# First image's state scan of a four-layer kernel: the product of delta*u and B on VectorE from PSUM instead of on GpSimd from a copy

## The reference

```
delta = softplus(dt @ W_dt.T + b_dt)          # 64 channels per pixel
A = -exp(A_log)                               # 64 channels x 16 states
...
dA = exp(d_t[..., None] * A)
h = dA * h + (d_t * u_t)[..., None] * B_t[:, None, :]
y = einsum('bdn,bn->bd', h, C_t)
...
y = (y + u * D) * silu(z)
return y @ W_out.T
```

## Time and profile before

| What | us |
|---|---|
| Three runs, median (lowest to highest) | 1260.89 (1253.15 to 1263.19) |
| Span of the profiled execution, first to last instruction | 1329.2 |
| First image's scan in it, first L1086 to the end of the last gate | 241.37 to 416.08 |
| Second image's scan, first L1026 to the last L1033 | 526.00 to 786.57 |
| First gather | 456.50 |
| Busy in the span: TensorE, VectorE, ScalarE, GpSimd | 611.3, 726.1, 269.3, 747.4 |

### The profile page before, as it was taken

The page is one execution under the profiler, slowest core; times in us unless marked ns, Lnnn a source line. Parts: engine busy times, 40 slices in busy tenths (PEclk is TensorE's granted clock), DMA queues, the critical chain, the costliest instruction groups (busy, mean ns, idle before and its releaser), DMA issues.

```text
span 1329.2 us, 7458 instructions
## 1 busy us (share of the span) xinstructions
PE 611.3 (46%) x1884; PEld 282.5 (21%) x1884; DVE 726.1 (55%) x894; ACT 269.3 (20%) x357; POOL 747.4 (56%) x627
## 2 busy tenths in 40 slices
PE   3414838667665755655657474341114112431115
PEld 1211213222221222222323221131002101220003
DVE  4989435899987556877878784081003101341004
ACT  1110137534441335121212111010001000110001
POOL 0325000444551278787877787567774775677770
PEclk9656879788787885787878786665556655575556
DMA  3000033000000511111111116222111111111110
GB/s 93 0 0 0 0 72 79 0 0 0 0 0 21 124 50 36 46 40 45 41 45 42 45 44 142 72 65 54 51 51 28 51 51 38 41 48 51 51 52 16
DMA packets 21877, 56.13 MB, mean 42 GB/s; under 512 B 10176, under 2 KB 10432, under 8 KB 20608
## 3 DMA queue, kind: packets, MB, share of 16 engines
q0 software_dynamic: 18432, 37.79, 10.6%
q1 hardware_dynamic: 2992, 16.76, 5.8%
q10 hardware_dynamic: 432, 1.33, 0.4%
HBM read 42.21 MB, written 5.24 MB: 36 GB/s over the span
## 4 chain that ended last, share of the span: by engine, by line
another core or an unknown queue 25%; POOL 21%; issue 14%; DVE 13%; PE 9%; ACT 3%; DMA 2%; ACTq 0%; POOLq 0%; DVEq 0%; SPq 0%
POOL got L733 19%; DVE scratch L1086 6%; PE PS L777 3%; PE PS L761 2%; ACT colT L767 1%; POOL got L1072 1%; DVE scratch L1091 1%; POOL scratch L1072 1%; DMA corner_table<-scratch 1%; PE PS L779 1%; PE PS L1108 1%; PE PS L984 1%; PE PS L841 1%; PE PS L842 1%
## 5 line engine op out<-in xcount | busy, mean ns | idle before, releaser
L733 POOL DMA_INDIRECT got<-corner_table,idx_slot x486 | 523.6, 1077 | 188.4 <-issue 146.6
L777 PE MATMUL PS<-colT,wt 128*32 128x128 f32 x512 | 95.4, 345 | 349.8 <-issue 208.6
L751 DVE TENSOR_TENSOR colg<-prodg 128x384 f32<-128x384 f32 x64 | 35.7, 558 | 305.8 <-remote 261.6
L984 PE MATMUL PS<-scratch,wt 128*128 128x512 f32 x256 | 161.9, 766 | 52.5 <-DVE scratch L1091 49.2
L777 PEld LDWEIGHTS PS<-colT,wt 128*32 128x32 f32 x512 | 64.4, 137 | 396.5 <-issue 307.2
L733 POOL DMA_INDIRECT got<-corner_table,idx_all x90 | 98.8, 1097 | 75.7 <-DMA corner_table<-scratch 48.5
L1072 POOL TENSOR_TENSOR scratch<-scratch 128x1024 f32<-128x1024 f32 x16 | 40.7, 2541 | 163.7 <-ACT scratch L1060 139.7
L969 PE MATMUL PS<-parts,selb 96*128 (+1 forms) x256 | 85.8, 449 | 97.4 <-DVE scratch L1026 62.0
L744 DVE TENSOR_TENSOR prodg<-got,coef 128x1152 f32<-128x1152 f32 x64 | 86.8, 1357 | 1.6
L984 PEld LDWEIGHTS PS<-scratch,wt 128*128 128x128 f32 x256 | 59.1, 241 | 122.1 <-DVE scratch L1091 64.5
L761 PE MATMUL PS<-mat,colg 128*128 128x128 f32 x256 | 56.9, 358 | 50.4 <-DVE colg L754 33.4
(11 more groups left out here) (304 smaller groups left out, 1018.6 us busy)
## 6 DMA issues: line engine op xcount, KB each, us to landing
got<-corner_table,idx_slot POOLq DMA_INDIRECT x486
XN<-ln_g SPq DMA_DIRECT2D x8, 256.0 KB, 5.1
corner_table<-scratch SPq DMA_DIRECT2D x1, 2048.0 KB
corner_table<-XN SPq DMA_DIRECT2D x1, 2048.0 KB
G<-XN SPq DMA_DIRECT2D x6, 256.0 KB
UZ<-scratch SPq DMA_DIRECT2D x6, 256.0 KB
got<-corner_table,idx_all POOLq DMA_INDIRECT x90
X<-in_x SPq DMA_DIRECT2D x4, 256.0 KB, 6.0
```

What stands on the lines that cost most here:

```text
L733: pool.indirect_dma_start(got[:, slot, tap, :, :].rearrange("p k c -> p (k c)"), None, tables[b], bass.IndirectOffsetOnAxis(ap=index[:, ta ...
L751: nc.vector.tensor_tensor(colg[:, 0:3 * P].rearrange("p (t k c) -> p t (k c)", k=2, c=C), prodg[:, 0:6, 0:2, :].rearrange("p t k c -> p t ...
L777: nc.tensor.matmul(PS[0:C, 7, 0:P], wt[:, W_L3 + C * r:W_L3 + C * r + C], colT[:, r * P:r * P + P], start=(r == 0), stop=False)
L984: last = nc.tensor.matmul(PS[:, 4 + n, :], wt[:, W_SUM:W_SUM + P], dBC[:, j % 2, n * BANK:(n + 1) * BANK], start=False, stop=(j == PAIRS - 1))
```

## The change

The first image's scan is now run by the functions of the second. The five `helped_` functions are gone. With them go GpSimd's 32 products, ScalarE's 32 copies of B, and the start of the scan before delta is complete: all four chunks of delta are finished first, and ScalarE and VectorE wait for them. No turns of the last layer are put in, since there are none yet. The second image's code stays as it is.

```diff
             low(0), left(2), low(1)
             between(2)
-            if b == 0:
-
-                project_delta(v, 0, 0)
-                left(3), low(2)
-                helped_du(v, 0)
-                low(3)
-            else:
-                left(3), low(2), low(3)
-                for c in range(NCHUNK):
-                    project_delta(v, 1, c)
+            left(3), low(2), low(3)
+            for c in range(NCHUNK):
+                project_delta(v, b, c)
             between(3)
...
             @block.gpsimd
             def _(pool):
-                with nc.gpsimd.Fori(0, NCHUNK) as i:
-                    helped_gpsimd(pool, i)
...
             @block.tensor
             def _(pe):
                 project_tensor(pe, 0)
-                pe.wait_ge(pr["parts_ready"], 1)
-                broadcast(pe, 0, 0, 0, 0, (pr["r_read"], 3))
                 pe.wait_ge(pr["parts_ready"], 4)
-                broadcast(pe, 0, 1, 0, 0, (sc["b_used"], 2))
-                broadcast(pe, 0, 0, 1, 2, None)
+                broadcast(pe, 0, 0, 0, 0, (pr["r_read"], 4))
                 with nc.tensor.Fori(0, NCHUNK - 1) as i:
-                    helped_tensor(pe, i)
-                helped_tensor(pe, NCHUNK - 1, ends=True)
+                    scan_tensor(pe, i, i)
+                scan_tensor(pe, NCHUNK - 1, NCHUNK - 1, ends=True)
                 output_tensor(pe, 0)
...
                 project_scalar(act, 0)
+                act.wait_ge(pr["delta_ready"], 4)
                 with nc.scalar.Fori(0, NCHUNK) as i:
-                    helped_scalar(act, i)
+                    scan_scalar(act, i, i)
...
                 project_vector(v, 0)
+                v.wait_ge(pr["delta_ready"], 4)
                 v.wait_ge(pr["parts_ready"], 4)
-                with nc.vector.Fori(0, NCHUNK - 1) as i:
-                    helped_vector(v, i)
-                helped_vector(v, NCHUNK - 1, ends=True)
+                with nc.vector.Fori(0, NCHUNK) as i:
+                    vchain.enter(i, 1)
+                    scan_vector(v, i, i)
+                vchain.leave(NCHUNK)
                 output_vector(v, 0)
```

More of the change, by code:

```diff
@@ L1036, in scan_vector @@
             gate(v, tok, c)
[L1041 to L1096, removed]
```

## The result

The changed kernel is slower by little: a median of 1263.49 us of eight runs (1260.96 to 1268.26) against 1258.93 us (1253.15 to 1263.19). The ratio is 1.0039, with a 95% interval of 1.0024 to 1.0055. The medians differ by 4.6 us, where 5 us were forecast.

The account below looks back on a forecast made before the run. VectorE's first scan, held up by GpSimd's products, was taken as the bound. Start and chunks came to 174.6 us against 174.7, so 0, plus 4.6 for TensorE's waits: about +5 us on 1260.9, 1266 us, range 1256 to 1277.

Parts of the forecast that it names:

- What bounds: First image's scan: VectorE's scan instructions stand still for GpSimd's products; GpSimd's help costs VectorE 40.5 us and saves 39.
- Part 1, the start: Before the first scan: four delta additions, then ScalarE's table load and first exponential, make it begin 2.9 us later.
- Part 2, a pair in time: Inside a chunk of the first scan: a pair takes 4.84 us on VectorE when TensorE is in time.
- Part 3, a chunk: First image's scan: three chunks of 43.6 us and a last of 41.0 to its gate, 171.7 us without TensorE's waits.
- the lost cover: At chunk starts: delta*u now stands behind the gate, no longer covered by TensorE's last additions; 1.43 us to the product.
- Part 4, TensorE: From pair to pair: at the half rate TensorE's additions make products late; 28 x 0.17 x 0.97 = 4.6 us.
- TensorE in time throughout: Rival, chance 0.22: the clock stays up within chunks of the first scan, so no waits; 0 us, 1261 us.
- TensorE becomes the bound: Rival, chance 0.15: the clock stays low from a chunk's start, TensorE's pair exceeds VectorE's; +20 to +27 us, 1285 us.
- Collisions worse: Rival, chance 0.08: GpSimd stretched the old scans 9 us more in unprofiled runs; change 4 us faster, 1257 us.
- The sum: Whole kernel: 0 + 4.6, about +5 us, giving 1266 us.
- the 68 us between span and median: Profiled span 1329.2 us against the runs' median 1260.9; taken not to touch the first scan, so the same 5 us added.
- one of the prediction's signs of being wrong: Stages behind the first scan: the prediction would be wrong if their length changed by more than 3 us.

Follow-up runs that it names:

- the fillers: Changed kernel plus five idle bf16 matmuls a pair on TensorE, results unread: stretch from last `low` row to last gate 180.9 us against 185.5; ratio 1.0001 to kernel before.

## Why the prediction was right

**What bounds.** Right, and shown: VectorE's scans were long because each was held until GpSimd's reading instruction ended. It also explains why the two kernels are so near each other. Before, a pair could not be shorter than GpSimd's product plus the scan, 2.35 + 2.35 us, as these exclude each other; now it is 4.83 us of VectorE alone.

**Part 1, the start.** 2.9 us forecast; 8.7 - 6.0 = 2.7 measured. The path was not quite the forecast one. It put ScalarE last, with VectorE's delta*u and product fitting beside it; VectorE's product ended last, by about 0.1 us. Counted from the last addition to the first scan, that is 2.95 us where ScalarE's path was put at 3.06, so the size hardly suffered.

**Part 2, a pair in time.** 4.84 forecast; 4.83 measured. The 32 scans of the first image take 2.35 us on average.

**Part 3, a chunk.** Chunks took 44.8, 44.6 and 44.2 us and the last 43.2 to its gate, where 43.6 and 41.0 plus waits were forecast. The term of the lost cover was right, as moving delta*u back shows.

**Part 4, TensorE.** The sum was right and its distribution was not. Forecast were 4.6 us of late products. From the first scan to the end of the last gate it is 176.8 us, 5.1 over the 171.7 without waits, and the fillers took 4.6 of it away. But only six products were late, by up to 0.5 us, 2.8 us together, where the forecast had 28 x 0.17 = 4.8 steps of 0.97 us. The other 2 us came at the chunk ends, which the forecast priced at the full rate (3.43 us from product to gate): there the gates' idle time is 10.8 us against 8.8 with the fillers. Nearly all of that, 1.7 us, is the last gate (3.88 against 2.19 us idle). TensorE has no next B to broadcast there, stands still, and adds the last states at the half rate:

```profile
413.20 3.68 PE L977 MATMUL PS<-scratch,wt 128*128 128x512 f32 x4 [2.51 <-DVE scratch L1026]
```

The two misses cancel, and that is luck: 4.6 us was the right sum of two wrong parts.

**The rivals.** *TensorE in time throughout* falls: the clock does drop within chunks, next section. *TensorE becomes the bound* falls: after each slow addition inside a chunk the next took 1.88 us again. *Collisions worse* falls: 102.9 us of scans in a second profile against 101.9, and the runs themselves got slower by 4.6 us, where this rival would have made them faster by 4.

**The sum.** 5 us forecast, 4.8 in the stretch, 4.6 in time. The guess that the 68 us between span and median don't touch the first scan was right for a reason I didn't have. The prediction thought of the profiler; the second profile of the kernel before shows an execution that is long by its run time (1327.41 us) as well as by its span (1325.6 us), on a chip where the median is 1321.37 us. So the chip makes the difference, most likely in the first profile too. For the same reason one of the prediction's signs of being wrong could not be read: the stages behind the scan went from 913 to 841 us between its two profiles, which the change did not do. The first scan began at 241.47 us and not at 244.3, because everything ahead of the last `low` came 2.6 us sooner in that profile; that part varies by as much between profiles of one kernel (VectorE's first L924 at 205.6, 207.9 and 205.8 us in three of the changed kernel).

## What to carry to other kernels

Before handing VectorE's work to GpSimd, look at what VectorE runs beside it. In these traces, where that had two SBUF inputs and GpSimd read SBUF, the two took turns; VectorE's products from PSUM overlapped freely. When a loop is replaced by a simpler shared one, list what the old one did under somebody's wait: here delta*u ahead of the gate was worth 4 to 5 us, as much as the whole loss, and keeping it needs no GpSimd. And an engine with slack on average can still make another late at single steps, so price its waits at both clock levels, the ends of a loop included.

## What was not expected of the hardware

**The clock falls without a long pause.** The changed kernel in three adjoining stretches (us, busy of PE, PEld, DVE, ACT, POOL, PEclk):

```profile
252.80:256.20 3.40, 1.50 (x5) 0.23 (x4) 3.33 (x5) 1.15 (x1) 0.00 (x0) 1.00 0.00 0
256.30:259.60 3.30, 3.30 (x6) 1.19 (x4) 3.27 (x3) 1.15 (x1) 0.00 (x0) 0.50 0.00 0
259.80:263.00 3.20, 2.25 (x8) 0.97 (x7) 2.85 (x2) 0.00 (x0) 0.00 (x0) 1.00 0.00 0
```

And what TensorE did there:

```profile
251.60 1.88 PE L977 MATMUL PS<-scratch,wt 128*128 128x512 f32 x4
254.86 0.60 PE L962 MATMUL PS<-parts,selb 96*128 x2 [1.38 <-DVE scratch L1026]
255.99 0.79 PE L962 MATMUL PS<-parts,selb 96*128 x2 [0.52 <-DVE scratch L1019]
256.57 3.44 PE L977 MATMUL PS<-scratch,wt 128*128 128x512 f32 x4
```

No pause was over 1.4 us, yet the granted clock went from 1.00 to 0.50, the addition took 3.44 us instead of 1.88, and the clock was back at 1.00 after it. TensorE had been busy for 1.50 of 3.40 us before the fall, and for all of 3.30 us before the rise. The same happened ten microseconds later, with the addition at 266.80 us. The pauses alone don't decide it: between 382 and 399 us the same pauses of 1.38 and 0.52 us repeat pair after pair with the clock at 1.00, and it falls only after 399.4 us. The Trainium skill, in "TensorE: Matmul & The Clock Gate", section "Why this matters for your kernels", advises against long idle gaps between bursts of matmuls. These chunks have none of that kind between their pairs, and the clock fell all the same, so following that advice was not enough here.

**The gather stages differ from chip to chip.** Everything behind the first scan took 841 us in the profile after (1259.2 - 418.25) and 908 to 916 us in the four other profiles of the two kernels, the one shown ahead of the prediction among them. Such a profile has rows like this one of the changed kernel on a second chip, with engines standing still for up to 36 us at a time:

```profile
1119.51 0.56 DVE L751 TENSOR_TENSOR colg<-prodg 128x384 f32<-128x384 f32 x1 [35.80 <-remote]
1120.09 1.92 PE L777 MATMUL PS<-colT,wt 128*32 128x128 f32 x8 [35.12 <-issue]
```

In that profile L751 waits 14 times for "remote", 237.4 us in all, in the one of the kernel before 261.6 us; in the profile after it never does. "Remote" says no more about the cause, and I made no run to find it. Such stops may also be why single executions scatter more on those chips, and why a change of 5 us was clear on the first chip and blurred on the others; that is not shown.
